# A transformer block on one Trainium2 core: the first two head groups' scores laid out on chip, the opening's work divided anew, and two DRAM buffers for the query and key rows

## The reference, cut to what matters

```python
x = L0_attn_x                                    # [16, 256, 128] float32
x = x + attn(layernorm(x), Wq, Wk, Wv, Wo)       # 16 heads, d_k = 8, d_v = 64, causal
x = x + moe(layernorm(x), gate_w, w1, w2)        # 8 experts, 64 tokens each, gelu

# attn, for each of 16 batches and 16 heads
q, k, v = x @ Wq, x @ Wk, x @ Wv
scores  = where(causal, -inf, q @ k.T / sqrt(8))
out     = softmax(scores) @ v @ Wo
```

## Time and profile before

| | |
|---|---|
| median of 3 runs | 535.07 us (534.59 to 536.13) |
| profiled execution | 537.27 us |
| its span | 535.5 us, 1.8 us less than its time |
| TensorE busy | 511.6 us, 96% of the span |
| VectorE, ScalarE, GpSimd busy | 79%, 74%, 49% |
| mean granted TensorE clock | 0.996 |
| DMA of `k_rows` into `k_diag`, 128 KB, issue to landing | 4.3 us, the page's median |
| ScalarE zeroing one part of `k_diag` (L548) | 1.05 us |
| TensorE's last own product; VectorE's first reading of it (L786) | starts 10.59; starts 11.05 |

### The profile page before, as it was taken

One profiled execution on the slowest core, in us unless ns is written; L12 is line 12 of the kernel. 1 busy time (PEld: TensorE's weight loads), 2 busy tenths in 40 slices (PEclk: granted clock), 3 DMA queues, 4 the chain that ended last, 5 costly groups with the idle time before them and its releaser, 6 DMA issues.

```text
span 535.5 us, 13983 instructions
## 1 busy us (share of the span) xinstructions
PE 511.6 (96%) x4783; PEld 424.9 (79%) x4783; DVE 423.9 (79%) x1081; ACT 398.1 (74%) x1379; POOL 264.3 (49%) x252
## 2 busy tenths in 40 slices
PE   2679999999999999999999999999999999999996
PEld 2458778788787787787787887877789999999996
DVE  6868889889888988889999999999974587644444
ACT  4788998989889898988989989899753643434330
POOL 8865565665655656656555655556920110011121
PEclk9989999999999999999999999999999999999999
DMA  5585152751733415132351423501300011100002
GB/s 165 152 223 148 36 137 81 237 147 26 191 106 83 124 32 157 52 104 80 80 159 35 127 80 79 156 4 46 95 21 1 2 33 58 32 12 21 11 23 59
DMA packets 49447, 45.71 MB, mean 85 GB/s; under 512 B 4208, under 2 KB 46192, under 8 KB 49392
## 3 DMA queue, kind: packets, MB, share of 16 engines
q1 hardware_dynamic: 48304, 44.14, 30.2%
q10 hardware_dynamic: 1088, 0.85, 0.6%
HBM read 26.09 MB, written 18.89 MB: 84 GB/s over the span
## 4 chain that ended last, share of the span: by engine, by line
PE 87%; DVE 5%; DMA 3%; issue 2%; ACT 2%; SPq 1%; POOLq 0%; POOL 0%; ACTq 0%; DVEq 0%
PE ctx_ps L1266 16%; PE t_ps L1353 10%; PE misc_ps L1275 10%; PE t_ps L1239 5%; PE t_ps L1240 5%; PE t_ps L1249 5%; PE misc_ps L1177 4%; PE s_ps L1337 4%; PE misc_ps L1179 3%; PE misc_ps L1178 3%; PE s_ps L1225 3%; PE s_ps L1338 3%; PE s_ps L1339 3%; PE s_ps L1212 3%; PE s_ps L1221 2%
## 5 line engine op out<-in xcount | busy, mean ns | idle before, releaser
L580 ACT ACTIVATE prob<-s_ps,neg_max 128x128 f32<-128x128 f32 (+1 forms) x512 | 210.6, 443 | 1.0 <-DVE neg_max L1051 0.7
L504 POOL TENSOR_TENSOR probn<-prob,inv 128x1024 f32<-128x1024 f32 x64 | 121.2, 1894 | 37.5 <-DVE inv L1072 37.4
L580 ACT ACTIVATION_READ_ACCUMULATOR prob<-s_ps,neg_max 128x1 f32 x512 | 117.7, 230 | 0.0
L497 POOL TENSOR_TENSOR probn<-prob,inv 128x512 f32<-128x512 f32 x64 | 66.6, 1041 | 69.9 <-PE t_ps L1249 68.9
L628 ACT ACTIVATE hT<-s_ps 128x512 f32<-128x512 f32 x64 | 38.1, 598 | 64.3 <-PE s_ps L1339 61.7
L1008 DVE TENSOR_REDUCE neg_max<-s_ps 128x4 f32<-128x1024 f32 x63 | 76.4, 1212 | 3.5 <-PE s_ps L1225 1.3
L533 POOL TENSOR_TENSOR y_parts<-y_sb,y_parts 128x512 fp32r<-128x512 f32 x16 | 21.2, 1326 | 106.9 <-ACT y_parts L638 106.9
L1275 PE MATMUL misc_ps<-wo_sb,ctxT 128*128 128x128 f32 x512 | 67.8, 275 | 0.7 <-DVE x_all L827 0.7
L1275 PEld LDWEIGHTS misc_ps<-wo_sb,ctxT 128*128 128x128 f32 x512 | 62.2, 192 | 1.1 <-issue 1.1
L1239 PE MATMUL t_ps<-ident,probn 128*128 128x128 f32 x256 | 61.7, 281 | 0.0
L1240 PE MATMUL t_ps<-ident,probn 128*128 128x128 f32 x256 | 60.1, 275 | 0.0
(11 more groups left out here) (198 smaller groups left out, 1178.5 us busy)
## 6 DMA issues: line engine op xcount, KB each, us to landing
qT<-q_rows SPq DMA_DIRECT2D x15, 512.0 KB, 4.0
q_rows<-qk_hi SPq DMA_DIRECT2D x32, 128.0 KB, 2.4
q_rows<-qk_lo SPq DMA_DIRECT2D x32, 128.0 KB, 2.4
k_diag_odd<-k_rows SPq DMA_DIRECT2D x32, 128.0 KB, 4.3
k_rows<-qk_hi SPq DMA_DIRECT2D x30, 128.0 KB, 2.4
k_rows<-qk_lo SPq DMA_DIRECT2D x30, 128.0 KB, 2.4
k_diag_even<-k_rows SPq DMA_DIRECT2D x28, 128.0 KB, 4.3
w_raw<-in_L_ffn_w SPq DMA_DIRECT2D x1, 2048.0 KB, 9.7
```

The source lines that it names most:

```text
L497: nc.gpsimd.tensor_tensor(probn[r][:, 0:HG * P].rearrange("p (i k) -> p i k", i=HG), prob[r][:, 0:HG * P].rearrange("p (i k) -> p i k", i=HG),
L504: nc.gpsimd.tensor_tensor(probn[r][:, HG * P:].rearrange("p (i k) -> p i k", i=HG), prob[r][:, HG * P:].rearrange("p (i k) -> p i k", i=HG ...
L580: last = nc.scalar.activation(prob[r][:, first + i * keys:first + (i + 1) * keys], scores[:, i, :], ACT.Exp, bias=neg_max[:, r, block_, i: ...
```

## The change

It does five things.

1. **Two units' layout on chip (OWN = 2).** The repeated weights hold eight heads. `first_own_product` (unit 0) runs before `queries_keys(0)`, `second_own_product` (unit 1) behind it. `split_own` and `own_rows` replace the old `split_own`: the selected keys are first made for all 128 rows, then four copies of 32 rows put them into `k_diag`, two by VectorE and two by ScalarE (unit 0) or GpSimd (unit 1, `own_keys`). Only units 2 and 3 of batch 0 come through DRAM.
2. **The opening's work divided anew.** Zeroing of `k_diag` moves: ScalarE takes both on-chip units' parts before anything else and one odd part, VectorE the other two even parts at its start and one odd, GpSimd two odd parts, the last of them in unit 1. GpSimd takes `wv_lo` (in halves) and the normalisation of batch 1 from VectorE; VectorE takes copies for the masks (`copy_half_masks`, `copy_half_rows`). The mask products of `second_scores(0)` run early (`mask_second`). GpSimd's `numbers` moves to unit 6.
3. **DMA queues.** Wk loads on SyncE's queue, ahead of x(1) and Wv. SyncE stores the low rows of batch 0's keys and makes all of its loads.
4. **Order behind unit 0.** TensorE makes unit 1's first scores before `queries_keys(1)`; VectorE's `split_qk(1)` moves from before the loop to inside unit 0, behind the refill of `s0_ps`.
5. **Two DRAM buffers** for rows: the stores of batch b wait for the loads of batch b-2.

```diff
-        q_rows = nc.dram_tensor("q_rows", [H, 4, DK, T], F32).ap()
-        k_rows = nc.dram_tensor("k_rows", [H, 4, DK, T], F32).ap()
+        q_rows = [nc.dram_tensor(f"q_rows{r}", [H, 4, DK, T], F32).ap() for r in range(RING)]
+        k_rows = [nc.dram_tensor(f"k_rows{r}", [H, 4, DK, T], F32).ap() for r in range(RING)]
...
             load_x(0)
+            sp.dma_start(wqk_raw[:, 1, :], w_k).then_inc(wqk_loaded[1], 16)
+            load_x(1)
             sp.dma_start(wv_raw[:, :], w_v).then_inc(wv_loaded, 16)
-            load_x(1)
...
             for b in range(B):
                 sp.wait_ge(qk_hi_done, b + 1)
-                await_count(sp, qk_loaded, QK_LOADS * b)
-                store_rows(sp, qk_hi, Q_HI)
+                await_count(sp, qk_loaded, QK_LOADS * (b - 1))
+                store_rows(sp, b, qk_hi, Q_HI)
...
# VectorE, the opening
+            zero_keys(0, 2)
             sign_copies()
+            zero_keys(0, 3)
             dve.wait_ge(x_loaded[0], 16)
             norm_stats(lambda tb: x_all[:, tb, :], bn6, mv1, bn1_done, 1, stats1)
+            first_var()
+            copy_half_rows()
             norm1(0)
             split_qk_weights()
             repeat_weights()
-            split_norms(0, 0)
+            split_norms(0, 0, t_ps[1])
+            copy_half_masks()
+            split_own(0)
+            own_rows(0)
+            split_qk(0)
             dve.wait_ge(x_loaded[1], 16)
...
             dve.wait_ge(exp1, 1)
             nc.vector.reciprocal(inv[:, 0, 1, :], sums[:, 0, 1, :]).then_inc(inv1, 1)
+            split_norms(1, 1, t_ps[1])
...
-            split_qk(1)
+            zero_keys(1, 0)
             batches(dve, batch)
...
# VectorE, in the loop, behind the refill of s0_ps
+                    if at(u, (0,)):
+                        split_qk(1)
...
# GpSimd, the opening
             mask_shapes()
-            norm1_scale(0)
-            pool.wait_ge(rstd1_done, 1)
+            first_scale()
+            zero_keys(1, 3)
             half_products()
-            norm1_scale(1)
...
+            split_values_weights(0)
+            second_norm()
+            split_values_weights(1)
+            own_keys()
             batches(pool, batch)
...
# ScalarE, the opening
+            zero_keys(0, 0, zeroed_own)
+            zero_keys(0, 1, zeroed_own)
+            split_qk_weights()
             repeat_weights()
...
+            split_own_keys()
             split_qk(0)
+            own_keys()
             act.wait_ge(qk_hi_done, 1)
-            store_rows(act, qk_hi, K_HI)
-            act.wait_ge(qk_lo_done, 1)
-            store_rows(act, qk_lo, K_LO)
-            zero_keys(0, 3, zeroed[0])
-            split_norms(1, 1, misc_ps[1])
+            store_rows(act, 0, qk_hi, K_HI)
+            zero_keys(1, 2, zeroed[1])
             act.wait_ge(max0, 1)
             exps(0, 0, s0_ps, P, 0, exp0)
...
+            split_norms(1, 1, t_ps[1])
             act.wait_ge(max1, 1)
             exps(0, 1, s1_ps, T, HG * P, exp1)
+            copy_values(0, 0, 0, misc_ps[1])
+            copy_values(1, 1, 0, t_ps[0])
             split_qk(1)
```

More of the change, by code:

```diff
@@ L43 @@
 LAST_PLACES_AT = 12
+OWN = 2
 GATHERED_AT = {1: (5,), 2: (6,), 3: (7,), 8: (12,), 9: (13,), 10: (14,), 11: (15,)}
@@ L216, in block_kernel @@
         x_loaded = [sem(f"x_loaded{i}") for i in range(len(XPARTS) - 1)]
-        wqk_loaded = sem("wqk_loaded")
+        wqk_loaded = [sem(f"wqk_loaded{w}") for w in range(2)]
         wv_loaded = sem("wv_loaded")
@@ L488, in batch @@
                     u, r = b * G + j, j % RING
-                    if j == 1 and has(b + 2, B):
+                    if j == 1 and has(b + 2, B) and not at(u, (1,)):
                         norm1_scale(b + 2)
+                    if at(u, (1,)):
+                        zero_keys(1, 1)
                     if j == 0 and has(b - 2, B):
@@ L549, in zero_keys, with split_qk_weights, split_own_keys, own_keys @@
                                      eps_sb[:, 0:1].broadcast_to([P, HG * T]), ACT.Copy, scale=0.0).then_inc(done, 1)
+            def split_qk_weights():
+                for w in range(2):
+                    act.wait_ge(wqk_loaded[w], 16)
+                    nc.scalar.activation(wqk_hi[:, w, :], wqk_raw[:, w, :], ACT.Copy,
+                                         scale=(DK ** -0.5 if w == 0 else 1.0)).then_inc(w_hi, 1)
+            def split_own_keys():
+                act.wait_ge(own_done, 2)
+                act.wait_ge(signs, 3)
+                nc.scalar.activation(own_hi[0][:, 1, :], own_ps[0][1], ACT.Copy, scale=hi_sign[:, 1:2]).then_inc(own_k_hi_done, 1)
+            def own_keys():
+                act.wait_ge(own_k_done, 1)
+                act.wait_ge(zeroed_own, OWN)
+                for i in range(2, HG):
+                    rows = slice(i * ROWS, (i + 1) * ROWS)
+                    last = nc.scalar.activation(k_diag[0][rows, 0, i, :], f32(own_hi[0][rows, 1, :]), ACT.Copy)
+                last.then_inc(own_keys_ready, 1)
             def repeat_weights():
@@ L1023, in batch @@
                             copy_probs(0, misc_ps[0][0:HALF, T:2 * T])
-                    if j == 0 and has(b + 2, B):
+                    if at(u, (0,)):
+                        split_qk(1)
+                    if j == 0 and has(b + 2, B) and not at(u, (0,)):
                         if isinstance(b, int) and b == 2:
@@ L1179, in split_product, with first_own_product, second_own_product @@
                 return nc.tensor.matmul(out_, w_l, x_h, start=False, stop=True)
-            def own_queries_keys():
+            def first_own_product():
+                part = slice(0, P)
                 pe.wait_ge(own_w, 4)
+                for weights in (own_w_hi, own_w_lo):
+                    for w in range(2):
+                        nc.tensor.matmul(own_ps[0][w], weights[:, w, part], xT_hi[0][:, :], start=weights is own_w_hi, stop=False)
+                pe.wait_ge(xT_ready, 1)
                 for w in range(2):
-                    last = split_product(own_ps[:, w, :], own_w_hi[:, w, :], own_w_lo[:, w, :],
-                                         xT_hi[0][:, :], xT_lo[0][:, :])
-                last.then_inc(own_done, 1)
+                    nc.tensor.matmul(own_ps[0][w], own_w_hi[:, w, part], xT_lo[0][:, :], start=False, stop=True).then_inc(own_done, 1)
+            def second_own_product():
+                part = slice(P, 2 * P)
+                for w in range(2):
+                    split_product(own_ps[1][w], own_w_hi[:, w, part], own_w_lo[:, w, part],
+                                  xT_hi[0][:, :], xT_lo[0][:, :]).then_inc(own_done, 1)
             def turn_first_norms(b, to=misc_ps[0]):
```

234 lines of the change are left out of this document (136 added, 98 removed).

## The result

| | before | after |
|---|---|---|
| median of the executions timed together | 535.22 us (534.52 to 538.24, 16) | 537.07 us (535.1 to 539.86, 16) |
| ratio to before, 95% interval | | 1.0037 [1.0022, 1.0052] |
| profiled execution, its span | 537.27, 535.5 | 538.69, 536.9 |
| first scores of unit 4 on TensorE | 37.53 | 38.16 |
| first load of batch 1 | 29.01 | 29.59 |

The change costs 1.85 us; I had forecast a gain of 0.9. Behind a median stand the range of its executions and, where it helps, their number. Two executions in a slower state of the chip are left out: one of a_qklo (579.41 us) and one of the kernel before beside it (836.03 us). The page of the profile after: span, and busy time by engine.

What follows compares the result with a forecast made beforehand. TensorE was taken to bound 37.5 to 350 us, so only an earlier start of unit 4, which waits for batch 1's keys over DRAM, would count. Loads 0.9 us early gave 535.07 - 0.9 = 534.2 us, range 533.5 to 535.0.

Steps and rivals of the forecast that it cites:

- What bounds the kernel now: 37.5 to 350 us: TensorE bounds; unit 4's start at 37.53 waits 2.50 us for batch 1's keys over DRAM.
- To xn: Opening on VectorE: xn takes 0.96 us beside GpSimd's zeroing and is done at 6.55, where it was 6.08.
- rival B: GpSimd's zeroing shuts VectorE out: xn ends at 9.0, everything 2.4 us later, 536.6 us; chance 0.09.
- To unit 0's and unit 1's scores: Opening on TensorE: unit 0's scores start at 11.8 (was 14.37), unit 1's near 18.3 (was 21.25).
- To queries and keys of batch 1: Behind unit 1's scores: `xT_lo` at 18.7, products 18.8, `qk_hi` 20.35, SyncE's first store 1.15 us early.
- The low rows give some back: Batch 1's stores: `qk_lo` ends at 23.7 and holds the fifth store, so loads start at 28.1, 0.9 us early.
- What costs nothing: Second DRAM buffer, GpSimd's `zero_keys(1, 1)` ahead of unit 1's `probn` (up to 2.9 us uncovered) and `numbers` cost nothing.
- What is late next: TensorE ahead of unit 4: arrives at about 32.8, finds keys at 36.6; the wait grows from 2.5 to 3.8 us.
- A: Longer wait ahead of unit 4 drops the clock: 535.9 us (short form) or 537.5 (long); chance 0.16, half each.
- C: Last key load lands 4.3 us after issue, unit 4 starts at 34.3, whole shift arrives: 531.9 us; chance 0.10.
- D: Chain starts earlier than thought: products of batch 1 at 18.4, stores 1.8 us early, 533.3 us; chance 0.10.
- E: No change: `qk_lo` of batch 1 is 0.9 us later still, 535.1 us; chance 0.10.

Runs made afterwards that it cites:

- a_qklo: Changed kernel with before's VectorE order: `split_qk(1)` ahead of unit 1's second maximum, `zero_keys(1, 0)` behind the refill in unit 0; 535.25 us, ratio 1.0010.
- a_again: The changed kernel, no edit, run again for a second trace; 538.3 us, ratio 1.0059 to the kernel before.
- b_qklo: The kernel before with only VectorE's `split_qk(1)` moved behind the refill in unit 0, zeroing not moved; 536.69 us, ratio 1.0040.
- b_again: The kernel before, no edit, run again for a second trace; 534.77 us, ratio 0.9995.
- b_warm3: The kernel before with ten filler products (results never used) on TensorE ahead of unit 0's first scores and ten ahead of unit 2's; 535.31 us, ratio 1.0008.
- b_xlate: The kernel before with SyncE loading the rest of x only once batch 1's queries and keys have landed; 534.96 us, ratio 1.0006.
- a_best2: a_best with `xT_lo` of batch 1 made ahead of the reciprocal that waits for the exponentials; 534.50 us, ratio 0.9998.
- a_lock: Changed kernel with GpSimd's `zero_keys(1, 3)` moved from ahead of the mask selections to behind the first half of `wv_lo`; 537.9 us, ratio 1.0044.
- a_one: Changed kernel with one DRAM buffer for rows and the old wait instead of two buffers; 536.47 us, ratio 1.0025.
- a_xlate: Changed kernel with SyncE loading the rest of x only once batch 1's queries and keys have landed; 536.33 us, ratio 1.0033.
- a_warm3: Changed kernel with filler products (results never used) on TensorE: 7 ahead of unit 1's first scores, 11 ahead of unit 2's, 12 ahead of unit 4's; 536.48 us, ratio 1.0030.
- a_best4: a_best3 with six more filler products ahead of unit 4's first scores; 535.21 us, ratio 1.0005.
- a_warm: Changed kernel with 12 filler products (results never used) on TensorE ahead of unit 4's first scores; 536.79 us, ratio 1.0034.
- a_best: Changed kernel with the edits of a_qklo and a_lock joined; 535.29 us, ratio 1.0022.
- a_best5: a_best2 with only six filler products, ahead of unit 4's first scores; 534.82 us, ratio 1.0009.
- a_best3: a_best2 with filler products on TensorE, 7 ahead of unit 1's first scores and 10 ahead of unit 2's; 536.75 us, ratio 1.0027.

## Why the prediction was wrong

**What bounds the kernel now: right in mechanism, wrong in size.** Unit 4's first scores were the point to watch, and the DMA round trip sets them. In all profiled kernels with full clock behind that point, the span ends 497.1 to 497.6 behind it, whatever was edited ahead of it, or 498.0 to 498.2 in the three with the long wait near 367 (before, a_again, b_qklo). But the 2.50 us of the earlier trace rows belonged to an execution 2.2 us slower than the median, whose last load took 6.54. I noted the difference and carried it over to the median instead of asking which row it sat in. In b_again's trace the wait is 0.52 (0.59 in b_warm3, none in b_xlate). From there the path is a near tie: a chain that starts earlier can gain only some 0.5 before `turn_last` at 34.96 takes over, unless that comes sooner too, as in a_best2 (33.40); one that starts later costs its full amount.

**To xn.** Predicted 0.96 for xn, measured 1.32, the repetition of the weights 1.32 instead of 0.65 (0.49 in a_lock). GpSimd's zeroing takes 2.79 and holds VectorE's work back, though not until its end: xn is done at 6.8 and not 9.0. With both, VectorE was some 0.95 later than forecast, and a_lock took 1.08 off unit 0's scores: rival B's mechanism was there at under half of its 2.4. The Trainium skill ("SBUF — State Buffer", Who interferes with whom) calls the shared port an exclusive lock; 1.32 against 0.60 agrees in direction, and the xn pair that ends 1.4 ahead of the zeroing doesn't agree with a lock that holds for the whole instruction.

**To unit 0's and unit 1's scores.** 13.28 instead of 11.8, and 19.16 instead of 18.3. The 32-row copies took 0.41 each on ScalarE, inside my bounds. a_lock, with 12.20 and 18.92, shows that most of the first miss is the stretching by GpSimd, and that little of it reaches batch 1 (0.2 at the low rows).

**To queries and keys of batch 1.** `xT_lo` was ready at 20.06 (predicted 18.7), products at 20.12 (18.8), `qk_hi` at 21.14 (20.35), first store 21.76: 0.35 early instead of 1.15. The reciprocal that `xT_lo` stands behind waited for the long exponentials of unit 0 until 19.58, and not until 18.2. I had seen this wait and sized it too small; a_best2 shows what `xT_lo`'s place behind it costs, 1.33 us at the first load.

**The low rows give some back: this is the step that failed.** I had `qk_lo` end at 23.7 and the loads 0.9 early; it ended at 24.97 and the loads started 0.58 late. Some 0.8 of the 1.27 came from the step before: unit 1's short exponentials, behind the late `qk_hi`, ended at 23.14 and not at 22.3. The other 0.5 is what I put at nothing without a reason. I counted the short exponentials, the reciprocal and the refill ahead of `qk_lo`, and not the two instructions that the order on VectorE shows there as well: `zero_keys(1, 0)`, 2.00 beside `probn`, and the second maximum of unit 1 behind it, 1.21. With them the reciprocal ran at 23.64, 0.5 behind the exponentials that it waits for. Before, the zeroing lay in a wait of VectorE and cost nothing; moved behind the first maximum it stood ahead of a maximum on which ScalarE, the refill and `qk_lo` all hang. b_qklo (+2.1 us) and a_qklo (-1.4 us) show that the place of `qk_lo` costs most of the loss; how much of it the zeroing adds isn't tested.

**The sum.** Between after's trace and b_again's the spans differ by 3.6 us: 0.61 at the first load, 1.41 in the last landing (6.60, not 5.19), 1.5 in the fall of the clock. Between a_again's and b_again's they differ by 1.6: 0.71 at the first load, less 0.11 in the last landing, 0.9 in the long wait near 367, and no fall. The loss in the medians, 1.85, lies between them.

**What costs nothing.** The second DRAM buffer: right (a_one). GpSimd's `zero_keys(1, 1)`, ahead of unit 1's `probn`, no run tests alone; the long `probn` there ended at 29.67 and not near 27.9.

**What is late next.** ScalarE's long exponentials of unit 1 start at 23.75 and not 22.3, for the same maximum; so `turn_last` came at 34.65, not 2.1 us early as I had put it, and the wait grew to 2.85 and not 3.8. The landing itself was as I said, 8.5 us behind the first load (29.59 to 38.11), and that was luck: in a_again's trace it is 7.0 (29.69 to 36.69), in b_again's 7.1.

**The rivals.** A came true in its result: the clock fell behind the wait ahead of unit 4, in its short form, one stretch of 3.4 us (forecast 1.7, measured 1.5). I had given A 0.16, half to each form. Its reason, that the idle is longer, didn't hold: it was 2.85 and not 3.8, and the clock fell after 1.59 in a_xlate and not after 1.90 in a_one or 2.50 in the earlier trace rows. That the measured 537.07 lies near the 537.5 of A's long form is chance: the rest of it comes from the chain. a_warm3 and a_best4 show no fall with fillers. Its size in the median of after is not settled: a_warm3's 1.0030 against after's 1.0037 and a_again's 1.0059 leaves 0.4 to 1.5 us, to which comes what the fillers themselves cost. C fell: the page's median landing is no guide, since unit 4 waits for the last of the four. D fell: the products came at 20.12, not at 18.4. E was the nearest for the chain: it had `qk_lo` 0.9 later still and no gain left, and `qk_lo` came 1.27 later.

**What stays open.** The last landing of key loads was 5.08 to 6.60 in the five chains with after's order (after 6.60, a_lock 6.37, a_one 5.91, a_xlate 5.87, a_again 5.08; with fillers a_warm 6.2, a_warm3 5.1) and 4.92 to 5.21 in the five with before's order in the changed kernel (a_best to a_best4 and a_qklo; a_best5 5.1). That isn't the order's doing alone: b_qklo, with the late order, had 4.84, and before's order had 6.54 in the first trace of before and 6.09 in b_warm3. a_xlate's 5.87 shows that it can be long without x's bytes; whether they add anything (b_xlate 4.6) these runs don't tell. Nor do they tell what makes the clock fall in some executions only.

## What to carry to other kernels

Before a wait of the trace goes into a sum, place the profiled execution among the timed ones: if it is 2 us above the median, take a second trace and look where the two differ, first in the wait that the argument rests on (here it held 1.4 of the 2.2). When an instruction moves, list everything that stands between its old neighbours and its new ones on its engine, and price each at what it takes beside what the other engines do then, not at what it took where it was hidden; ask as well what it holds up that others wait for. An opening that speeds up the engine which is the bound later, but not the transfer that it waits for, buys a longer wait. Here a fall of the clock came behind such waits in some executions and cost 1.5 us.

## What the hardware showed unexpectedly

- VectorE instructions stretch beside GpSimd ones: the pair xn 0.60 to 1.32, two copies of 32x256 from 0.85 to 1.78, one zeroing of 128x1024 from 0.68 to 2.00. Near 365 us the same xn pair took 1.56 in some traces and 2.44 in others of the same kernel, and TensorE waited 0.88 longer behind the second.
- The same DMA round trip differs between executions and kernels with the same bytes: the last store's landing 2.33 to 3.70 us, that of the last of four key loads 4.6 to 6.6. In a_xlate about one of 16 DMA engines was still busy at the end of a landing of 5.87.
- Where TensorE waited 1.6 to 2.9 us ahead of unit 4, the clock fell to 1.2 GHz 0.1 to 1.4 us after it had resumed dense work, and not during the wait (after, a_xlate, a_lock); from unit 4's first scores to unit 5's took 7.5 to 7.6 us then, and 6.0 without a fall. After 1.90 in a_one's trace and 1.99 in a_best3's it didn't fall, nor after 2.50 in the earlier trace rows. The length of the one wait doesn't decide it alone.
